# Attention layer of a macaron block: out-projections, stores, loads and layer norms at other ticks of a software pipeline, and one product with values issued later

## The reference

```
x = x + 0.5 * ffn(layernorm(x))
x = x + attention(layernorm(x))      # returns its own residual as well
x = x + 0.5 * ffn(layernorm(x))

attention(x): h = layernorm(x) * ln_scale + ln_bias
  c_q, c_kv = h @ w_down_q.T, h @ w_down_kv.T                      # 256 -> 128
  q, k = rope(c_q @ w_up_q.T), rope(c_kv @ w_up_k.T); v = c_kv @ w_up_v.T   # 16 heads of 64
  out = softmax(q k^T / 8) v ; return out @ w_out.T + x
```

## Time and profile before

| | us |
|---|---|
| median of 3 runs | 4161.7 |
| lowest and highest | 4150.89, 4165.04 |
| the profiled execution | 4144.14 |
| its span | 4142.2 |
| PE busy | 3935.1 |
| POOL busy | 2955.7 |
| DVE busy | 2790.7 |
| ACT busy | 2630.8 |

### The profile page before, as it was taken

How to read it: one execution, slowest core, us unless ns; L and a number is a source line. 1 busy time by engine, 2 the same in 40 slices (tenths; PEclk the granted TensorE clock), 3 DMA queues, 4 the chain that set the end, 5 groups by cost and what they waited for, 6 DMA issues and landing times. The chain is left out here.

```text
span 4142.2 us, 65717 instructions
## 1 busy us (share of the span) xinstructions
PE 3935.1 (95%) x24908; PEld 2209.9 (53%) x24908; DVE 2790.7 (67%) x3709; ACT 2630.8 (64%) x3276; POOL 2955.7 (71%) x1634
## 2 busy tenths in 40 slices
PE   7999979999999999999999999999999999989999
PEld 6888834444444444444444444444444444468888
DVE  5665567777767776776777667767777777556563
ACT  4545447766766676667667766766676667645544
POOL 3444448878878887878788888878887888634443
PEclk9999989999999999999999999999999999989999
DMA  3333221112211211121122122111211121132331
GB/s 108 112 123 101 87 92 52 55 57 65 71 59 52 73 62 52 58 82 52 52 66 72 55 63 73 58 54 57 78 61 52 52 83 55 40 122 96 123 113 62
DMA packets 192771, 300.36 MB, mean 73 GB/s; under 512 B 50327, under 2 KB 100936, under 8 KB 191816
## 3 DMA queue, kind: packets, MB, share of 16 engines
q1 hardware_dynamic: 192456, 296.17, 22.3%
HBM read 201.20 MB, written 26.73 MB: 55 GB/s over the span
## 5 line engine op out<-in xcount | busy, mean ns | idle before, releaser
L1078 DVE TENSOR_REDUCE atNM<-atPS 128x2 f32<-128x1024 f32 x1024 | 1229.6, 1221 | 520.8 <-PE atPS L889 519.5
L1019 ACT ACTIVATE atPT<-atPS 128x1024 f32<-128x1024 f32 x1024 | 1036.1, 1020 | 581.6 <-PE atPS L910 573.4
L1177 POOL TENSOR_TENSOR atACC<-atACC,atPT 128x1024 f32<-128x1024 f32 x510 | 1243.7, 2439 | 85.6 <-ACT atPT L1019 35.5
L921 PE MATMUL atPO<-atPT,atV 128*64 128x512 f32 x4096 | 1030.5, 606 | 26.5 <-ACT atAT L1026 26.1
L1010 ACT ACTIVATE atPS<-atSH 128x1024 f32<-128x1024 f32 x768 | 779.0, 1024 | 182.9 <-DVE atNM L1078 149.7
L1177 POOL TENSOR_TENSOR atACC<-atPT 128x1024 f32<-128x1024 f32 x255 | 609.4, 2390 | 242.3 <-PE atOT L943 142.8
L921 PEld LDWEIGHTS atPO<-atPT,atV 128*64 128x64 f32 x4096 | 255.4, 137 | 478.4 <-issue 391.1
L910 PE MATMUL atPS<-atQH,atKL 64*128 64x512 f32 x2048 | 457.1, 443 | 46.1 <-ACT atPS L1010 35.2
L889 PE MATMUL atPS<-atKH,atQH 64*128 64x512 f32 x2048 | 456.4, 443 | 20.8 <-ACT atQH L999 15.3
L910 PE MATMUL atPS<-atQL,atKH 64*128 64x512 f32 x2048 | 405.8, 392 | 0.0
L910 PE MATMUL atPS<-atQH,atKH 64*128 64x512 f32 x2048 | 405.7, 392 | 0.0
(11 more groups left out here) (278 smaller groups left out, 6511.9 us busy)
## 6 DMA issues: line engine op xcount, KB each, us to landing
atSH<-atMD SPq DMA_DIRECT2D x128, 512.0 KB, 4.4
atVT<-atR SPq DMA_DIRECT2D x508, 128.0 KB, 2.1
f1GB<-f1GD SPq DMA_DIRECT2D x128, 256.0 KB, 6.9
f2GB<-f2GD SPq DMA_DIRECT2D x128, 256.0 KB, 6.9
atRSUM<-atRD SPq DMA_DIRECT2D x126, 256.0 KB, 4.0
X<-x SPq DMA_DIRECT2D x4, 1024.0 KB, 5.7
XS<-x SPq DMA_DIRECT2D x16, 256.0 KB, 3.8
x<-X SPq DMA_DIRECT2D x16, 256.0 KB, 3.0
```

The lines of the kernel that those rows point to most:

```text
L921: ins = pe.eng.matmul(PO[HI[h], :], V[n % 2][:, j, HI[h]], PT[k % NPT][:, h, :], start=j == 0, stop=j == T - 1)
L1019: act.eng.activation(PT[k % NPT][:, :, :], PS[ring.of[step]][:, :, :], ACT.Exp, scale=SCALE).then_inc(grown.sem)
L1078: dve.eng.tensor_reduce(NM[:, q // 4, :, q % 4, t], PS[ring.of[step]][:, :, :], AX.X, ALU.max, negate=True).then_inc(most_out.sem)
L1177: pool.eng.tensor_tensor(total[:, :, :], begun[:, :, :], PT[k % NPT][:, :, :], ALU.add).then_inc(gathered.sem)
```

## The change

The four quarters of `outward` move from periods 24, 24, 27 and 28 to 24, 31, 31 and 32, each given with its table. The stores move by 2, 5, 4 and 2 periods. The loads follow a store's period by 4 instead of by 3 or 2. `stats`, `spread` and `norm` move 5, 5 and 4 periods later. At a half boundary the first attend of the next half is held over (`held`) and written into the next group, behind its score, most, score and the other steps of its first tick; and at a half boundary the other steps of tick x+1 now come ahead of the half's last attend. `gathers` is the former filter as a function.

```
                         for i in range(4):
-                            at(end, m, -40 + i, ("stats", b, i))
+                            at(end, m, -35 + i, ("stats", b, i))
                         for k in range(T):
-                            at(end, m, -33 + k, ("norm", b, k))
-                        at(end, m, -36, ("spread", b))
+                            at(end, m, -29 + k, ("norm", b, k))
+                        at(end, m, -31, ("spread", b))
...
                 if p % GP == GP - 1:
-                    for u, (period, table) in enumerate([(24, early), (24, late), (27, late), (28, late)]):
+                    for u, (period, table) in enumerate([(24, late), (31, early), (31, late), (32, early)]):
                         at(table, m, period, ("outward", m, u))
                 if p == NP - 1:
-                    for u, period in enumerate((25, 26, 28, 30)):
+                    for u, period in enumerate((27, 31, 32, 32)):
                         at(end, m, period, ("store", b, u))
                         if b + 2 < NB:
-                            at(end, m, period + 3 - u // 2, ("load", b + 2, u))
+                            at(end, m, period + 4, ("load", b + 2, u))
...
+            def gathers(attends):
+                return [("gather",) + s[1:] for s in attends if s[3] % 4 and s[1:3] + (s[3] // 4,) != (NN - 1, 1, 1)]
...
-            order = []
+            order, held = [], []
             for x in range(-42, 2 * PER * (NN + 4), 3):
                 order += tile("score", x) + most_of(x) + tile("fill", x + 2) + tile("score", x + 1)
-                order += others_of(x) + tile("attend", x - 1)
-                order += [step for step in tile("gather", x - 1) if step[3] % 4 and step[1:3] + (step[3] // 4,) != (NN - 1, 1, 1)]
+                order += others_of(x) + held + tile("attend", x - 1)
+                order += gathers(held + tile("attend", x - 1))
                 order += most_of(x + 1) + tile("score", x + 2) + most_of(x + 2)
-                if x % T == T - 1:
-                    order += tile("fill", x + 3) + tile("attend", x) + others_of(x + 1) + tile("fill", x + 4) + tile("attend", x + 1)
-                else:
-                    order += tile("fill", x + 3) + others_of(x + 1) + tile("fill", x + 4) + tile("attend", x) + tile("attend", x + 1)
-                order += [step for i in range(2) for step in tile("gather", x + i)
-                          if step[3] % 4 and step[1:3] + (step[3] // 4,) != (NN - 1, 1, 1)] + others_of(x + 2)
+                now, held = tile("attend", x), tile("attend", x + 1)
+                if x % T < T - 1:
+                    now, held = now + held, []
+                order += tile("fill", x + 3) + others_of(x + 1) + tile("fill", x + 4) + now + gathers(now) + others_of(x + 2)
```

## The result

The changed kernel takes 4132.4 us at the median of four runs (4129.4 to 4134.7), the kernel before 4157.9 (4150.9 to 4165.0): a ratio of 0.9938, with a 95% interval from 0.9918 to 0.9958. On another chip, with six and 29 runs, it was 0.9952 (0.9939 to 0.9966). So it is 20 to 25 us faster, where 14 were forecast.

A forecast was written before the change was run, and what follows sets the result against it. The prediction took PE to bound the kernel. Gains of 55 us (16 + 12.7 + 26) less losses of 41 (4 + 13 + 20 + 4) gave 14 us less, 4147 against the median 4161.7, with a range of 4118 to 4170.

The forecast's parts named there:

- The half boundaries, 63 above a multiple of 96: At 11 half boundaries without a step between the attends, PE's 1.77 us wait for ACT's copy goes: gain 16 us.
- The boundaries at 15: At 11 half boundaries where an outward stands between the attends: next to nothing to win.
- The boundaries at 39 and 87: At 21 half boundaries with a raise between the attends, PE waits for DVE's fill instead: loss 21 x 0.2 = 4 us.
- The division: PE's 7 waits for POOL's division before the first outward vanish as the spread moves behind it: gain 12.7 us.
- The cover: Outwards moved to periods 31 and 32 fill PE's idle time while ACT catches up: gain 26 us.
- The vacated places: Groups that outwards leave lose cover and wait for DVE's or ACT's fill: loss 13 us, bounds 0 and 20.
- The bank atOT: Turns and latents directly behind outwards wait for DVE's addition, 0.95 us, 21 times: loss 20 us.
- The rival in which the bank decides: Each outward ahead of a turn or latent costs 2.2 us, not 0.95: 14 us more, 4176; chance 0.13.
- cover without price: Rival: bank collisions cost PE little and vacated places stay quiet: 35 us less, 4127; chance 0.22.
- The tail: At the end, pair 61's three outwards come later and the last sum 7 us later: loss 4 us, bounds 1.7 and 7.
- The sum: Whole kernel: gains 55, losses 41, so 14 us less, 4147 against the median; chance 0.40.
- an idle PE that doesn't fall: Sign of being wrong: PE's idle time in the attention stage falls by more than 30 us or not at all.

The follow-up runs named there:

- experiment 3: Kernel before with only the new order at half boundaries (attend held, other steps ahead of the last attend): 4149.3 us, ratio 0.9992 to before.
- experiment 4: Changed kernel with the old order at half boundaries, nothing held; outwards, stores, loads and norms still moved: 4154.4 us, ratio 1.0011 to before.
- experiment 2: Kernel before with only stats, spread and norm moved later: 4140.6 us, ratio 0.9978 to before.
- experiment 1: Changed kernel run again without an edit, beside the kernel before: 4129.8 us against 4151.4, ratio 0.9952.
- the second trace: Profile of the unaltered changed kernel taken in experiment 1; attention 3025.6 us.
- experiment 8: Changed kernel with each batch's first outward alone back at period 24, early: 4117.8 us, ratio 0.9909 to before.
- experiment 9: Changed kernel with DVE's fill ahead of the other steps of tick x+1 at half boundaries alone: 4122.7 us, ratio 0.9930 to before.
- experiment 5: Changed kernel with the four outwards of each batch's second odd pair at their old ticks, none ahead of a turn or latent: 4116.3 us, ratio 0.9901 to before.
- experiment 10: Changed kernel with the edits of experiment 5, experiment 8 and experiment 9 together, and pair 61's outwards at old ticks: 4091.2 us, ratio 0.9845 to before.
- experiment 7: Changed kernel with the loads of quarters 2 and 3 two periods later, away from the inverse: 4140.1 us, ratio 0.9961 to before.
- experiment 6: Changed kernel with DVE's fill ahead of the other steps of tick x+1 in every fourth group: 4179.0 us, ratio 1.0051 to before.

## Why the prediction was right in sign and too small, step by step

**The half boundaries, 63 above a multiple of 96: wrong in the place of the gain.** I wrote that PE does score, most, score first, and gains the 1.77 us. The first of these scores had no filled bank: ACT's chain of exponential, fill, high part and copy was itself the late one, and experiment 3 gives 0.29 us for 1.77. I had followed ACT's copy and DVE's fill and not ACT's fill. The 16 us of this step came all the same in the changed kernel (5.31 of work for 2.65), but from the outwards that now stand there, with or without hold (+2.65 and +2.60).

**The boundaries at 15: wrong in the reason.** "Next to nothing to win" is true of the kernel before, where an outward separates the attends. The change takes it away, and hold is what makes that free: -1.98 with, 0.00 without. Alone, hold takes 3 us (experiment 3, within its interval of nothing) and the moved outwards add 14 (experiment 4 against 2). Both together take 11 us, the difference between experiments 1 and 2 (0.9952 - 0.9978). I had priced both edits against the kernel before and added them. The sum was hardly hurt: I had neither the 1.77 us that an outward leaving without hold gives away here nor the hold that saves it, and together they come to 0.2 us a place.

**The boundaries at 39 and 87: right.** I had 0.2 us of loss each and DVE's fill as the late step. Measured with hold alone: +0.10 and +0.31. The new timeline at the place of the earlier trace rows:

```profile
2413.49 1.23 DVE L1080 TENSOR_REDUCE atNM<-atPS 128x2 f32<-128x1024 f32 x1 [0.55 <-PE atPS L891]
...
2414.64 0.68 DVE L1061 TENSOR_TENSOR atR<-atOT,atSIN 128x512 f32<-128x512 f32 x1
...
2415.23 0.68 DVE L1064 TENSOR_TENSOR atU<-atOT,atCOS 128x512 f32<-128x512 f32 x1
...
2415.83 1.22 DVE L1086 COPY atPS<-atSH 128x1024 f32<-128x1024 f32 x1
...
2417.10 0.50 PE L912 MATMUL atPS<-atQH,atKL 64*128 64x512 f32 x2 [0.66 <-DVE atPS L1086]
```

From the reduction's start to the fill's end it is 3.56 us, where the working gave 2421.3 - 2417.72 = 3.58. DVE runs the four without a gap, and PE, which had no such wait before, stands 0.66 us.

**The division: right**, 12.7 us of waits gone. By itself the edit gives 9 us (5 to 13).

**The cover: right, at ticks 30 to 36 too small.** Predicted 1.15 us there; both traces give 5.31 - 3.80 = 1.51 or a little more, as rows of idle time leave out what starts show. For 93 to 3 I predicted 1.84; the second trace gives 5.31 - 3.01 = 2.30 and the first 1.43, so it stays open. With the third stretch's 2.66 the three are 5.6 to 6.5 us in a repeat.

**The vacated places: right where a row was read, too small elsewhere.** Ticks 54 and 57 lost 0.80 (0.60 forecast), 78 to 84 lost 0.42 (0.44). But 48 and 51 lost 1.24, for which I had 2 us in all over 11 repeats, and 87 and 90 lost 1.10, of which I had 0.2. The first was the high part behind an outward, experiment 8; I had looked at the score ahead of that outward and not at the most behind it. Of the second, experiment 9 gives back 0.7 by letting DVE fill first. Together they lost 13 + 12 us, where the sum held 2 in all for the first and 0.2 a place for the second.

**The bank atOT: right**, in count and mechanism. 21 waits of 0.79 us; 0.95 forecast. From one batch, the first outward, the turn right behind it, and the turn and the latent behind the next two outwards; each of the three waits for DVE's addition:

```profile
2375.01 1.95 PE L963 MATMUL atOT<-atWO,atAT 128*64 128x256 f32 x16
2377.75 0.66 PE L852 MATMUL atOT<-ident,Y 128*128 128x128 f32 x4 [0.79 <-DVE X L1118]
...
2383.46 0.66 PE L852 MATMUL atOT<-ident,Y 128*128 128x128 f32 x4 [0.79 <-DVE X L1118]
...
2388.50 1.98 PE L860 MATMUL atOT<-atHT,WDq 128*128 128x512 f32 x4 [0.79 <-DVE X L1118]
```

The rival in which the bank decides, at 2.2 us each, did not come: no addition stood behind a fill. Nor did "cover without price": experiment 5, which undoes these collisions, took 21 us.

**The tail: right.** The last sum was to come 7 us later after the sum ahead of it:

```profile
3593.42 1.94 PE L938 MATMUL atOT<-atACC,atones 128*64 128x512 f32 x8
...
3598.82 1.95 PE L963 MATMUL atOT<-atWO,atAT 128*64 128x256 f32 x16 [1.75 <-DVE atRSUM L1097]
...
3607.06 1.08 PE L938 MATMUL atOT<-atACC,atones 128*64 128x512 f32 x4
```

That is 13.6 us, 7.1 more than the 6.57 from this row of the trace of before to the 3616.31 of the earlier trace rows, and the wait for the reciprocal is 1.75, as worked out.

```profile
3609.74 1.94 PE L936 MATMUL atOT<-atACC,atones 128*64 128x512 f32 x8
```

From tick 960 to the end the second trace is 1.9 us longer than before: 4 forecast, the lower bound 1.7.

**The sum: right in part by luck.** The trade of cover and of hold came out at 20 us over the repeats by one trace of the changed kernel and 32 by the other, the bank takes 17 back, the division gives 9 to 13, the tail takes 2. That is 10 to 26 us less by steps, against 20 to 25 measured and 14 forecast. The clock stands in no step, and some 5 to 10 us of the difference are likely its (last section), so the steps don't close more tightly than this. By the second trace two groups of errors largely cancelled in each repeat: the three stretches into which the outwards moved came out 1.7 us better than priced (0.9 of it at 60 to 66), and the places that outwards left, at 48, 54 and 87, 2.2 us worse. And one sign that I had named for being wrong, an idle PE that doesn't fall, came near: it fell by 2 us in the first trace and 7 in the second, where 14 were forecast.

## What to carry to other kernels

In an order written out by hand, price each moved step against the order that results and not against the old one: here one edit was worth nothing alone and 24 us beside another, since the second opened the wait that the first closes. When a wait is taken away, follow every engine's chain to the next instruction of the busiest one (fills by both engines, high parts, additions), for the wait that is next is often only half a microsecond shorter. And look at steps that share one bank wherever two periodic patterns meet; 21 adjacent pairs cost as much as the whole change gained.

## What the runs showed of the hardware

TensorE's granted clock fell from 2.4 to 1.2 GHz, for 3.4 us at a time and rarely 6.8, at places in the attention that differed between the two traces of the changed kernel. A fall in its first trace, with PE's wait just ahead of it and the windows before and in it, and then the same ticks in the second trace (columns as in the earlier trace rows):

```profile
2437.95 0.57 PE L891 MATMUL atPS<-atKH,atQH 64*128 64x512 f32 x2 [1.01 <-ACT atQH L1001]
```

```profile
2428.00:2436.00 8.00, 7.60 (x48) 3.09 (x44) 4.85 (x5) 6.49 (x9) 6.55 (x4) 1.00 0.20 64
2436.00:2442.00 6.00, 4.99 (x26) 2.75 (x28) 3.20 (x3) 4.23 (x5) 5.86 (x4) 0.72 0.00 0
```

```profile
2422.00:2428.00 6.00, 5.83 (x36) 2.40 (x32) 3.57 (x3) 5.18 (x6) 5.86 (x4) 1.00 0.03 12
```

PE had been busy 7.6 of the 8 us to 2436. Then it waited 1.01 us, to 2437.95, and the clock fell 0.3 us later. The two groups there take 3.0 us longer than in the second trace; the other three falls in the two traces of the changed kernel cost 0.7 to 1.5 us each.

The places are not random. The twelve traces have 52 falls between the attention's first score and its last outward through `atOT`, and at each of them PE had a wait of 1.0 to 3.0 us that ended within 2 us of the fall's start, ahead of it or behind. Not every such wait has a fall: the changed kernel's second trace has 26 of at least 1.0 us and two falls. The count goes roughly with the time, though it is that of one trace each and the medians are from several chips:

| trace | falls in the attention | median us |
|---|---|---|
| experiment 10 | 0 | 4091.2 |
| experiment 8 | 1 | 4117.8 |
| changed kernel, twice | 2, 2 | 4132.4, 4129.8 |
| experiments 5 and 9 | 3, 3 | 4116.3, 4122.7 |
| before; experiment 7 | 5; 5 | 4157.9; 4140.1 |
| experiments 3 and 4 | 6, 6 | 4149.3, 4154.4 |
| experiment 2 | 7 | 4140.6 |
| experiment 6 | 12 | 4179.0 |

This suggests that a long wait of PE that an order takes away is worth more than its length, and that one that it makes costs more. For the change itself: the mean granted clock of the whole program is 0.984 over the 29 executions of before and 0.986 over the six of the changed kernel on that chip. Taken to four digits the means are 0.9838 and 0.9862, and 0.0024 of 4142 us are 10 us of PE's time; the traces gave 5 us. I estimate from these that 5 to 10 of the 20 to 25 us come by way of the clock. No experiment held the clock apart from the waits, so this is argued and not shown. Executions of one kernel differ by 3 us (experiment 10) to 29 us (before), and of the 29 of before the slowest had the lowest clock, 0.980, and the fastest the highest, 0.987, so a part of that is likely the falls' too. It also means that the difference of two single traces, 9.4 us here between the first of each, is not the change's.
